# Clipping the feed-forward weights on GpSimd instead of VectorE inside one attention tile

## The chip, the cores and the metric

The kernel runs on one core of one Trainium2 chip. The metric is the time of one execution on the device in microseconds; lower is better. The time before is the median of three runs.

## The reference, cut to what matters

One transformer-like layer over x of 16 sequences × 64 tokens × 256: cross attention with 16 heads to a context of 256 tokens per sequence, then a selective-scan (Mamba) layer, then a gated feed-forward layer whose weights are quantised to −1, 0, 1. The change touches only how those weights are prepared.

```python
def _weight_quant(w):
    scale = 1.0 / jnp.clip(jnp.mean(jnp.abs(w)), 1e-05)
    wq = jnp.clip(jnp.round(w * scale), -1.0, 1.0) / scale
    return w + jax.lax.stop_gradient(wq - w)
...
gate = jax.nn.silu(_bitlinear(x, w_gate))      # w_gate, w_up: 1024 x 256
up = _bitlinear(x, w_up)
return _bitlinear(gate * up, w_down)           # w_down: 256 x 1024
...
x = x + _L0_xattn_ref(_layernorm(x, axis=-1), ctx_1024, ...)
x = x + _L0_attn_ref(_layernorm(x, axis=-1), ...)
x = x + _L0_ffn_ref(_layernorm(x, axis=-1), L0_ffn_w_gate, L0_ffn_w_up, L0_ffn_w_down)
```

## The kernel before

The program is written out by hand: each engine has its own instruction queue, run strictly in order, and semaphores tie the queues together. There are three stages. In the first, eight attention tiles (t = 0 to 7) of 128 tokens each run one after the other; in the second, the selective scan runs over 64 half units (GpSimd's `weigh`, VectorE's `scan`); in the third, the feed-forward layer runs over eight tiles.

An attention tile has eight units (u = 0 to 7), two heads for two sequences each. The work of one unit goes round the engines:

- TensorE computes the scores (`scores`, L496), VectorE masks them and takes the largest (`mask_scores`, L1425), ScalarE takes the exponential and its sum (`exps`, L1016), VectorE inverts the sums (`invert_sums`, L1432) one unit later.
- GpSimd multiplies the probabilities by the inverse (`normalise`, L1843), two instructions of 128x256 for each unit. TensorE turns them (`turn_probs`, L513), also one unit later; VectorE or ScalarE copies them to SBUF (`copy_pt`, L1437 and L1022), TensorE multiplies them with the values (`values`, L531).

Between the units each queue has other work at fixed places: on TensorE the keys (`keys`, L544), queries and values of the next tile, the projection of the previous one (`project`, L584) and the turn of its normalised output (`scan_in`, L596). The first key projection of the next tile is issued at unit 0, which is what marks a tile's start in the text. On VectorE stand the layer norms' statistics (L1373, L1377) and second halves (`ln_second`, L1381), in which GpSimd computes the inverse deviation between the two (`rstds`, L1826 and L1829). `rstds` stands before the normalise of unit 2, 4 and 6. GpSimd also adds the bias of the projection (`add_bias`, L1836) and the residual (`pool_resid`, L1864) at unit 6.

The feed-forward weights are three arrays of 128x2048 float32 in SBUF (`wraw`). They are prepared in the shadow of the attention, in six halves of 128x1024, one half behind each of units 1 to 6 of a tile: absolute sums on ScalarE in tile 2 (`W_SUM`), the mean in tile 3, scaling and rounding (adding MAGIC) on ScalarE in tile 4 (`scale_weights`, L1069), the clip in tile 5 (`W_CLIP`, `clip_weights`, L1532), the conversion to bfloat16 on ScalarE in tile 6 (`weights_to_bf16`, L1074). Before the scan stage, several queues wait for all six conversions (`w_step`).

Of the kernel before, what the change touches and what calls it, by code (L numbers as in the profile page):

```python
# [17 lines left out]
ALU = mybir.AluOpType  # L18
# [24 lines left out]
MAGIC = 12582912.0  # L43
# [27 lines left out]
W_SUM, W_MEAN, W_SCALE, W_CLIP, W_BF16 = 2, 3, 4, 5, 6  # L71
# [35 lines left out]
def build(nc, x, ctx_t, mask, wq, wkv, wproj, bproj, vecs, cons, win, wall, wout, wg, wu, wd, out):  # L107
    with ExitStack() as ctx:
# [5 lines left out]
        def sem(name, by=None):  # L114

            s = ctx.enter_context(nc.semaphore(name))
            if by is not None:
                from_one[by].append(s)  # L120
            return s
# [50 lines left out]
        def first_use(at, n):  # L172
            return both[:, at:at + n]
# [8 lines left out]
        wraw = [first_use(16384 + 2048 * n, 2048) for n in range(3)]  # L182
# [38 lines left out]
        HALF_W = KD * FI // 2  # L221

        def half_of(w, n):
            return w[:, HALF_W * n:HALF_W * (n + 1)]
# [75 lines left out]
        w_scaled, w_clipped = sem("w_scaled"), sem("w_clipped")  # L300
# [49 lines left out]
        def lagged(tile, u, lag, first, fn, only=None):  # L350

            v = u - lag
            if v >= UNITS or v < 0 and first:
                return
            if only is None or v % UNITS in only:
                fn(tile if v >= 0 else tile.step(-1), v % UNITS)
# [632 lines left out]
        def _(act):  # L989
# [80 lines left out]

            def weights_to_bf16(n):

                act.wait_ge(w_clipped, n + 1)
                act.activation(half_of(wq3[n // 2], n % 2), half_of(wraw[n // 2], n % 2), ACT.Copy, bias=-MAGIC  # L1074
                               ).then_inc(w_step, 1)

# [284 lines left out]
        def _(dve):  # L1361
# [6 lines left out]
            def ln_first(n, tile, src, src_sem, src_val):  # L1368

                if src_sem is not None:  # L1370
                    dve.wait_ge(src_sem, count(src_val))
                dve.wait_ge(ln_mv[n], count(tile.t))
                dve.bn_stats(stats[n][:], src).then_inc(ln_stats[n], 1)  # L1373
                dve.wait_ge(ln_rstd[n], count(tile.t))
                dve.wait_ge(ln_stats[n], count(tile.t + 1))
                dve.sem_inc(passed, 1)
                dve.bn_aggr(meanvar[n][:], stats[n][:]).then_inc(ln_mv[n], 1)  # L1377
# [26 lines left out]
            def copy_vals(tile):  # L1404
                dve.wait_ge(v_ready[1], count(tile.t + 1))
                dve.wait_ge(pv_done, count(tile.t * 2 - 2))
                dve.tensor_copy(v_sb[:, tile.par, 1].rearrange("p k d -> p (k d)"), bank(6)).then_inc(v_in_sb[1], 1)
# [9 lines left out]
            def mask_scores(tile, u):  # L1417

                dve.wait_ge(s_ready, count(tile.t * 8 + (u + 1)))
                if u == 0:  # L1420
                    dve.wait_ge(maskf_ready, count(tile.t + 1))
                dve.wait_ge(pt_ready, count(tile.t * 8 + (u - 7)))
                dve.sem_inc(passed, 1)
                for q in range(2):
                    dve.tensor_tensor_reduce(sm[:, u, q * LK:(q + 1) * LK], score_bank(tile, u)[:, q * LK:(q + 1) * LK],  # L1425
                                             maskf[:, tile.par, q * LK:(q + 1) * LK], 1.0, HUGE, ALU.add,
                                             ALU.min, negmax[:, u, q:q + 1]).then_inc(masked, 1)
# [38 lines left out]
            def body(tile, first, last):  # L1466
                nxt, prev = tile.step(1), tile.step(-1)
                for u in range(UNITS):
                    if last:
                        if u % 2 == 0 and u:  # L1470
                            mask_scores(tile, u)
                            mask_scores(tile, u + 1)
                    else:
                        if u in MASK_AT:
                            for v in MASK_AT[u]:
                                mask_scores(tile, v)
                        if u == UNITS - 1:
                            mask_scores(nxt, 0)
                            if nxt.last():
                                mask_scores(nxt, 1)  # L1480
                    lagged(tile, u, LAG_INVERT, first, invert_sums)
                    lagged(tile, u, LAG_COPY_ODD, first, copy_pt, (1, 3, 5, 7))
                    if first and u == 0:
                        copy_vals(tile)
                        dve.wait_ge(loaded, N_LOADED)
                    if not last:
                        if u == DVE_LN1_FIRST:
                            ln_first(0, nxt, x_of(nxt), None, 0)
                        if u == DVE_LN1_SECOND:
                            ln1_second(nxt)  # L1490
                        if u == DVE_KEYS:
                            copy_keys(nxt)
                        if u == DVE_QUERIES:
                            copy_queries(nxt)
                        if u == DVE_VALS:
                            copy_vals(nxt)
                    if not first:
                        if u == DVE_PICK_HEADS + last:
                            pick_heads(prev)
                        if u == DVE_ADD_PROJ + last:  # L1500
                            add_proj(prev)
                        if u == DVE_NORM_Y1 + last:
                            norm_y1(prev)
                        if u == DVE_NORM_Z:
                            norm_z(prev)
                    if u == DVE_MASK and not last:
                        make_mask(nxt)
                    if last:
                        for c in range(NC):
                            if u == CONVOLVE_AT[c]:  # L1510
                                convolve(0, c)
                    if first and u == 6:
                        late_constants()
                    if tile.t == W_MEAN and u == 5:
                        dve.wait_ge(w_sum, 1)
                        dve.tensor_copy(wpart[:], bank(4)[:, 0:6]).then_inc(w_mean, 1)
                        dve.wait_ge(w_mean, 1)
                        dve.tensor_reduce(wmean[:], wpart[:].rearrange("p (n h) -> p n h", h=2), AX, ALU.add
                                          ).then_inc(w_mean, 1)
                        dve.wait_ge(w_mean, 2)  # L1520
                        dve.tensor_scalar(wmean[:], wmean[:], 1.0 / (D * FI), EPS, ALU.mult, ALU.max
                                          ).then_inc(w_mean, 1)
                        dve.wait_ge(w_mean, 3)
                        dve.reciprocal(winv[:], wmean[:]).then_inc(w_inv, 1)
                    if tile.t == W_CLIP and 1 <= u <= 6:
                        clip_weights(u - 1)

            def clip_weights(n):

                dve.wait_ge(w_scaled, n + 1)  # L1530
                part = half_of(wraw[n // 2], n % 2)
                dve.tensor_scalar(part, part, MAGIC + 1.0, MAGIC - 1.0, ALU.min, ALU.max  # L1532
                                  ).then_inc(w_clipped, 1)

            def late_constants():
                dve.tensor_copy(identb[:], ident).then_inc(consts, 1)
# [284 lines left out]
        def _(pool):  # L1821
# [16 lines left out]
            def normalise(tile, u):  # L1838
                pool.wait_ge(rden_ready, count(tile.t * 8 + (u + 1)))
                pool.sem_inc(passed, 1)  # L1840
                for q in range(2):
                    s = sm[:, u, q * LK:(q + 1) * LK]
                    pool.tensor_scalar(s, s, rden[:, u, q:q + 1], 1.0, ALU.mult, ALU.mult).then_inc(normed, 1)  # L1843

            def body(tile, first, last):
                nxt, prev = tile.step(1), tile.step(-1)
                for u in range(UNITS):
                    if u == POOL_RSTD0 and not last:
                        rstds(0, nxt)
                    if u == 2 and first:  # L1850
                        pool.wait_ge(loaded, N_LOADED)
                        add_bias(tile)
                    if u == POOL_BIAS and not last:
                        add_bias(nxt)
                    if u == POOL_RSTD1 and not first:
                        rstds(1, prev)
                    if u == POOL_RSTD2 + last and not first:
                        rstds(2, prev)
                        pool_resid(prev)
                    normalise(tile, u)  # L1860

            def pool_resid(tile):
                pool.wait_ge(ln_out[1], count(tile.t + 1))
# [214 lines left out]
```

## Time and profile before

| what | before |
|---|---|
| runs: median (lowest to highest) | 410.5 us (409.54 to 410.86) |
| profiled execution: span, its own time | 410.8 us, 412.68 us |
| TensorE matmuls busy | 361.4 us (88%) |
| VectorE busy | 348.2 us (85%) |
| ScalarE busy | 278.7 us (68%) |
| GpSimd busy | 285.5 us (69%) |
| mean granted clock of TensorE | 0.992 |

The span is from the first to the last instruction of the profiled execution; its own time includes what lies around them. Busy times are means over the whole span, with stages of quite different limits: the attention takes the first 180 us or so, the scan goes on to some 365 us, and the feed-forward layer follows.

### The profile page before, as it was taken

The numbers are of one execution on the slowest core, as the hardware profiler recorded it, in microseconds if no ns is written. First come the engines' busy times: TensorE is split into PE (matmuls) and PEld (weight loads), VectorE is DVE, ScalarE is ACT, GpSimd is POOL, SyncE is SP. The second block draws the span as 40 slices with busy tenths as digits, with TensorE's granted clock in tenths as the row PEclk, the third lists the DMA queues.
The fourth block names the chain that finished last, engine by engine and source line by source line (L and its number), as shares of the span: only waits on it lengthen the run. The fifth ranks groups of instructions, "written<-read, shape, count | busy, mean of one in ns | idle before, by whom it ended". The sixth has DMA issues, their size and how long they took to land.

```text
span 410.8 us, 8698 instructions
## 1 busy us (share of the span) xinstructions
PE 361.4 (88%) x2886; PEld 246.2 (60%) x2886; DVE 348.2 (85%) x723; ACT 278.7 (68%) x596; POOL 285.5 (69%) x333
## 2 busy tenths in 40 slices
PE   7899999999998999887798999898889778889774
PEld 5556767676776765453465566566576656557442
DVE  1558888797989778958989999989999999988795
ACT  1267589769966993489569879857874554266574
POOL 0056475565657472248999999999999699986830
PEclk9999999999999999999699999999999999999999
DMA  7981010110100000019400001364000000000001
GB/s 209 357 360 53 2 51 14 42 51 3 53 2 0 2 3 0 2 38 249 128 2 0 2 4 26 92 191 129 2 1 2 1 2 0 2 0 2 14 26 65
DMA packets 23039, 22.41 MB, mean 55 GB/s; under 512 B 1074, under 2 KB 20914, under 8 KB 22484
## 3 DMA queue, kind: packets, MB, share of 16 engines
q1 hardware_dynamic: 22436, 21.39, 16.7%
q8 instruction: 23, 0.38, 0.4%
q10 hardware_dynamic: 560, 0.48, 0.4%
q14 instruction: 20, 0.16, 0.1%
HBM read 20.75 MB, written 1.12 MB: 53 GB/s over the span
## 4 chain that ended last, share of the span: by engine, by line
PE 28%; DVE 20%; ACT 17%; POOL 17%; issue 16%; DMA 1%; DVEq 0%; PEld 0%; POOLq 0%; SPq 0%; ACTq 0%; PEldq 0%
POOL both L1897 12%; PE ps L544 7%; ACT both L1181 5%; DVE both L1601 4%; PE ps L513 4%; PE ps L496 3%; DVE both L1425 2%; PE ps L531 2%; PE ps L607 2%; PE ps L574 2%; ACT both L1016 2%; PE ps L759 2%; PE ps L561 2%; DVE f_s L1693 1%; ACT both L1167 1%
## 5 line engine op out<-in xcount | busy, mean ns | idle before, releaser
L1897 POOL TENSOR_TENSOR both<-both 128x1024 f32<-128x1024 f32 x64 | 150.4, 2386 | 2.4 <-DVE both L1601 1.8
L1601 DVE TENSOR_TENSOR_SCAN both<-both,ps 128x1024 f32<-128x1024 f32 x64 | 143.0, 2271 | 5.6 <-PE ps L749 5.5
L1843 POOL TENSOR_SCALAR both<-both,rden 128x256 f32<-128x256 f32 x128 | 61.7, 497 | 62.8 <-DVE rden L1432 62.6
L1181 ACT ACTIVATE both<-delta,a_neg 128x504 f32<-128x504 f32 x120 | 74.8, 704 | 12.3 <-DVE both L1601 12.2
L759 PE MATMUL ps<-con,both 128*128 128x128 f32 x512 | 72.5, 281 | 7.5 <-POOL both L1897 7.4
L759 PEld LDWEIGHTS ps<-con,both 128*128 128x128 f32 x512 | 56.8, 142 | 29.5 <-issue 16.3
L1016 ACT ACTIVATE both<-both,negmax 128x256 f32<-128x256 f32 x128 | 63.3, 498 | 15.7 <-DVE negmax L1425 15.7
L749 PE MATMUL ps<-both 32*128 32x256 f32 x512 | 46.7, 435 | 11.7 <-DVE both L1601 9.6
L1425 DVE CUSTOM_DVE_ANT_0 both<-ps,both 128x256 f32<-128x256 f32 x128 | 46.9, 417 | 6.7 <-PE ps L496 5.5
L513 PEld LDWEIGHTS ps<-con,both 128*128 128x128 f32 x256 | 30.6, 141 | 12.7 <-issue 8.0
L513 PE MATMUL ps<-con,both 128*128 128x128 f32 x256 | 38.2, 275 | 0.0
L749 PEld LDWEIGHTS ps<-both 32*128 32x128 f32 x512 | 20.5, 186 | 27.6 <-DVE both L1601 15.5
L544 PE MATMUL ps<-both 128*128 128x512 f32 x64 | 33.0, 640 | 2.7 <-DMA both<-in_wkv 1.3
L574 PE MATMUL ps<-both 128*128 128x256 f32 x128 | 31.1, 387 | 0.5 <-DVE both L1400 0.5
L1437 DVE COPY both<-ps 128x512 f32<-128x512 f32 x32 | 21.6, 676 | 10.2 <-PE ps L513 10.2
L1022 ACT ACTIVATE both<-ps 128x512 f32<-128x512 f32 x32 | 18.8, 588 | 14.6 <-PE ps L513 14.6
L574 PEld LDWEIGHTS ps<-both 128*128 128x128 f32 x128 | 23.1, 190 | 6.0 <-issue 2.7
L1016 ACT ACTIVATION_READ_ACCUMULATOR both<-both,negmax 128x1 f32 x128 | 24.5, 191 | 0.0
L1826 POOL TENSOR_TENSOR vareps<-meanvar,eps 128x1 f32<-128x1 f32 x24 | 6.3, 261 | 25.5 <-DVE meanvar L1377 25.5
L496 PE MATMUL ps<-both 32*128 32x256 f32 x256 | 20.6, 399 | 3.0 <-DVE negmax L1425 2.0
L544 PEld LDWEIGHTS ps<-both 128*128 128x128 f32 x64 | 11.3, 197 | 14.9 <-issue 13.0
L496 PEld LDWEIGHTS ps<-both 32*128 32x128 f32 x256 | 13.2, 184 | 8.3 <-issue 6.7
(151 smaller groups left out, 616.7 us busy)
## 6 DMA issues: line engine op xcount, KB each, us to landing
both<-bounce SPq DMA_DIRECT2D x16, 512.0 KB, 6.4
both<-in_ctx_t SPq DMA_DIRECT2D x8, 512.0 KB, 3.4
both<-in_wg SPq DMA_DIRECT2D x1, 1024.0 KB, 8.9
both<-in_wu SPq DMA_DIRECT2D x1, 1024.0 KB, 10.6
both<-in_wd SPq DMA_DIRECT2D x1, 1024.0 KB, 12.6
win_sb<-in_win SPq DMA_DIRECT2D x1, 1024.0 KB, 13.8
resid<-in_x SPq DMA_DIRECT2D x1, 896.0 KB, 6.3
both<-in_wkv SPq DMA_DIRECT2D x2, 256.0 KB, 3.4
```

The lines of the kernel that those rows point to most:

```text
L496: mm = pe.matmul(score_bank(tile, v)[:, bb * LK:(bb + 1) * LK], q2[rows, tile.par, hf, bb].rearrange("p r q -> p (r q)"), kt_sb[rows, tile ...
L513: tr = pe.transpose(pt_bank(tile, u)[:, (q * 2 + kt) * P:(q * 2 + kt + 1) * P], sm[:, u, q * LK + kt * P:q * LK + (kt + 1) * P], ident)
L544: mm = pe.matmul(kv_bank(tile, hf), wkv_sb[:, k, hf * P:(hf + 1) * P], ctx_sb[:, tile.par, k], start=k == 0, stop=k == KD - 1)
L574: mm = pe.matmul(kv_bank(tile, 1 - bb)[:, kt * D:(kt + 1) * D], ctx_sb[:, tile.par, k, bb * LK + kt * P:bb * LK + (kt + 1) * P], wkv_sb[:, ...
L749: mm = pe.matmul(bank(inflow_bank(hu) + sq).rearrange("p (n h t) -> p n h t", n=HN, h=2)[:, :, th], ut[rows, e.idx % 2, tt], bd[rows, e.nh ...
L759: mm = pe.matmul(bank(Y_BANK)[:, e.tt * P:(e.tt + 1) * P], g_sb[:, hu % RING_G, n * P:(n + 1) * P], ident, start=False, stop=e.nh == NH - ...
L1016: act.activation(s, s, ACT.Exp, scale=-1.0, bias=negmax[:, u, q:q + 1], accum_out=den[:, u, q:q + 1]).then_inc(expd, 1)
L1181: act.activation(da[sl % 2].rearrange("p (a s n t) -> p a s n t", a=GT, n=HN, s=2)[:, :, :, n, 1:L], delta[:, idx % RING_D].rearrange("p ( ...
L1425: dve.tensor_tensor_reduce(sm[:, u, q * LK:(q + 1) * LK], score_bank(tile, u)[:, q * LK:(q + 1) * LK], maskf[:, tile.par, q * LK:(q + 1) * ...
L1601: dve.tensor_tensor_scan(h_sb[:, hu % RING_H], da[e.slot % 2][:, e.tt * HU:(e.tt + 1) * HU], bank(inflow_bank(hu), 2), 0.0, ALU.mult, ALU. ...
L1843: pool.tensor_scalar(s, s, rden[:, u, q:q + 1], 1.0, ALU.mult, ALU.mult).then_inc(normed, 1)
L1897: pool.tensor_tensor(g_sb[:, hu % RING_G].rearrange("p (n s t) -> p s n t", n=HN, s=2), h_sb[:, hu % RING_H].rearrange("p (s n t) -> p s n ...
```

## The change

VectorE no longer clips. GpSimd does, behind its normalise of units 1 to 6 of the same tile (5). Each half of 1024 columns is clipped by two instructions of 512 columns, so the semaphore `w_clipped` counts 12 instead of 6, and ScalarE waits for twice the count plus two. The arithmetic is the same.

```diff
             def weights_to_bf16(n):
 
-                act.wait_ge(w_clipped, n + 1)
+                act.wait_ge(w_clipped, 2 * n + 2)
...
-                    if tile.t == W_CLIP and 1 <= u <= 6:
-                        clip_weights(u - 1)
-
-            def clip_weights(n):
-
-                dve.wait_ge(w_scaled, n + 1)
-                part = half_of(wraw[n // 2], n % 2)
-                dve.tensor_scalar(part, part, MAGIC + 1.0, MAGIC - 1.0, ALU.min, ALU.max
-                                  ).then_inc(w_clipped, 1)
...
                     normalise(tile, u)
+                    if tile.t == W_CLIP and 1 <= u <= 6:
+                        clip_weights(u - 1)
+
+            def clip_weights(n):
+
+                pool.wait_ge(w_scaled, n + 1)
+                part = half_of(wraw[n // 2], n % 2)
+                for q in range(2):
+                    quarter = part[:, HALF_W // 2 * q:HALF_W // 2 * (q + 1)]
+                    pool.tensor_scalar(quarter, quarter, MAGIC + 1.0, MAGIC - 1.0, ALU.min, ALU.max
+                                       ).then_inc(w_clipped, 1)
```

## Rows read from the trace of the kernel before

**Rows 1.** The page's first part: busy time, share of the span, instructions.

```profile
PE 361.4 (88%) x2886; PEld 246.2 (60%) x2886; DVE 348.2 (85%) x723; ACT 278.7 (68%) x596; POOL 285.5 (69%) x333
```

**Rows 2.** Windows, tiles 4 and 5: length, busy PE PEld DVE ACT POOL, clock, DMA.

```profile
93.05:112.01 18.96, 18.23 (x169) 13.09 (x169) 16.01 (x62) 18.16 (x48) 11.42 (x25) 1.00 0.10 30
112.01:132.04 20.03, 18.26 (x169) 13.12 (x169) 18.67 (x68) 12.61 (x42) 12.90 (x24) 1.00 0.01 1
```

**Rows 3.** VectorE's clip by source line: duration in ns min/median/max, first and last start.

```profile
L1532 DVE TENSOR_SCALAR both<-both x6: 659/668/1219, 113.0 to 127.7; 128x1024 f32<-128x1024 f32 x6
```

**Rows 4.** The chain of waits in tile 5: start us, us on it, what.

```profile
119.82 0.68 DVE both L1532
...
123.00 0.38 DVE both L1532
...
125.08 0.59 DVE both L1532
...
127.79 0.35 DVE both L1532
```

**Rows 5.** GpSimd's timeline, tile 5 and start of 6: start us, us, [idle before, releaser].

```profile
113.30 2.09 POOL L1843 TENSOR_SCALAR both<-both,rden 128x256 f32<-128x256 f32 x4 [0.42 <-DVE rden L1432]
115.86 0.54 POOL L1826 TENSOR_TENSOR vareps<-meanvar,eps 128x1 f32<-128x1 f32 x1 [0.47 <-DVE meanvar L1377]
...
120.78 0.93 POOL L1843 TENSOR_SCALAR both<-both,rden 128x256 f32<-128x256 f32 x2 [1.84 <-DVE rden L1432]
...
127.42 0.90 POOL L1836 TENSOR_TENSOR resid<-resid,both 128x256 f32<-128x256 f32 x1
...
129.00 0.55 POOL L1829 TENSOR_TENSOR rstd<-vareps,neg_half 128x1 f32<-128x1 f32 x1
129.52 0.73 POOL L1864 TENSOR_TENSOR resid<-y,z 128x256 f32<-128x256 f32 x1
...
132.21 0.93 POOL L1843 TENSOR_SCALAR both<-both,rden 128x256 f32<-128x256 f32 x2 [0.94 <-DVE rden L1432]
...
135.89 0.19 POOL L1826 TENSOR_TENSOR vareps<-meanvar,eps 128x1 f32<-128x1 f32 x1 [0.50 <-DVE meanvar L1377]
```

**Rows 6.** VectorE's timeline in tile 5.

```profile
122.87 0.18 DVE L1377 BATCH_NORM_AGGREGATE meanvar<-stats 128x2 f32<-128x6 f32 x1
...
124.92 0.08 DVE L1425 DVE_READ_ACCUMULATOR2_ANT negmax<- 128x1 f32 x1
...
127.65 1.22 DVE L1532 TENSOR_SCALAR both<-both 128x1024 f32<-128x1024 f32 x1
```

**Rows 7.** TensorE's timeline where tile 5 ends and tile 6 begins.

```profile
130.61 0.44 PE L596 MATMUL ps<-con,xn 128*128 128x128 f32 x2 [0.94 <-DVE xn L1381]
...
132.04 1.95 PE L544 MATMUL ps<-both 128*128 128x512 f32 x4
133.83 0.60 PE L513 MATMUL ps<-con,both 128*128 128x128 f32 x4
```

**Rows 8.** GpSimd's two-operation instructions by source line: ns min/median/max, starts, forms.

```profile
L1843 POOL TENSOR_SCALAR both<-both,rden x128: 471/478/736, 20.5 to 177.8; 128x256 f32<-128x256 f32 x128
...
L1965 POOL TENSOR_SCALAR xnt<-xnt,f_s x5: 474/478/481, 369.8 to 392.1; 128x256 f32<-128x256 f32 x5
...
L1938 POOL TENSOR_SCALAR dtb<-xnt x8: 1065/1070/1537, 340.3 to 392.7; 128x256 bf16<-128x256 f32 x8
...
L1932 POOL TENSOR_SCALAR xnt<-resid,f_s x5: 1217/1218/1219, 366.9 to 387.9; 128x256 f32<-128x256 f32 x5
```

**Rows 9.** Groups of GpSimd by form: one column, and two inputs of 504 columns.

```profile
L1906 POOL TENSOR_TENSOR xc<-xc,zst 128x504 f32<-128x504 f32 x4 | 5.1, 1263 | 0.0
...
L1921 POOL TENSOR_SCALAR f_nmean<-f_s 128x1 f32<-128x1 f32 x3 | 0.8, 265 | 0.3
```

**Rows 10.** Windows of the stretch where TensorE's granted clock falls.

```profile
188.00:192.00 4.00, 1.63 (x12) 0.54 (x10) 3.76 (x6) 4.00 (x12) 3.43 (x7) 1.00 1.07 286
...
196.00:200.00 4.00, 1.88 (x11) 1.23 (x12) 4.00 (x3) 1.76 (x4) 3.94 (x2) 0.70 0.88 237
```

## The prediction, made before the change was run

> **What bounds the kernel now.** I read the page's busy shares first: no engine is saturated over the span; TensorE and VectorE lead and GpSimd stands at 69% [rows 1]. That share is a mean, and the change lives in one attention tile, so I cut the span there: from one tile's first key projection to the next is 18.96 us in tile 4 and 20.03 us in tile 5, the clip tile [rows 2]. TensorE does the same 18.2 us of work in both; what differs is VectorE, 16.01 us busy against 18.67. The chain of waits says why: four of the six clips stand on it in tile 5, for 0.68, 0.38, 0.59 and 0.35 us, 2.0 us together [rows 4]. So VectorE's clips do set the pace of tile 5, and the most that their removal can give there is about what tile 5 has over tile 4, 20.03 − 18.96 = 1.07 us. Then I read the timeline of the engine that gets the work. GpSimd is busy 12.90 of tile 5's 20.03 us [rows 2], so it has 7.1 us free, in gaps of 0.4 to 1.8 us where it waits for VectorE [rows 5]. Last, TensorE at the seam: its turn of the probabilities of unit 7 starts at 133.83, and GpSimd's normalise of that unit ends at 132.21 + 0.93 = 133.14 [rows 5, 7]. That is the slack of GpSimd at the seam: 0.7 us. Whatever pushes that normalise more than 0.7 us delays TensorE, and with it tile 6 and everything behind it, because every engine's queue runs in order and the attention tiles lead into the scan.
>
> **What is removed.** Six clips on VectorE, 668 ns each in the median, one of 1219 [rows 3]. That one starts at 127.65, while GpSimd's add of the bias runs from 127.42 to 128.32 [rows 5, 6], so some 0.6 us of it is waiting for that instruction. The reverse is seen too: GpSimd's one-column add at 115.86 takes 0.54 us against 0.19 at 135.89 in tile 6, where there is no clip [rows 5]. Both losses go. The Trainium skill ("SBUF — State Buffer", section "Who interferes with whom") says that GpSimd and a VectorE instruction in a two-port mode exclude each other for a whole instruction; the trace agrees with that here, and by it VectorE's short SBUF-to-SBUF instructions could now wait behind a clip piece. I cost that at nothing, since the sum below has VectorE ahead of GpSimd anyway.
>
> **What is added.** Twelve instructions on GpSimd, 128x512 float32 in place, minimum then maximum with two constants, a pair behind the normalise of each of units 1 to 6. No such form is in the trace, so I bound it. Four forms with two operations on 256 columns stand there: multiply then multiply, 478 ns; multiply then add, 478 ns; subtract then minimum, constants, bfloat16 out, 1070 ns; subtract then multiply, 1218 ns [rows 8]. One column takes 265 ns [rows 9], which I take as the fixed part. Doubling the rest: 265 + 2 × 213 = 691 ns on the fast forms, 265 + 2 × 805 = 1875 ns and 265 + 2 × 953 = 2171 ns on the slow ones. The fast forms hold only multiply and add. The only one with a minimum, and the only one with two constants, is slow. So I take the slow side, between its two: 2.0 us a piece, 4.0 us a pair, 24 us in all, and keep 0.69 us as the other end.
>
> The Trainium skill speaks against this choice ("GPSIMD Engine Reference", section 3.1, "Elementwise — side-by-side cycle accounting"): a loop body with at most two operations is bound by its port at 1.03 cycles per element. My estimate from that page of the Trainium skill is 512 × 1.03 / 1.2 GHz = 440 ns and a start, near the fast end. The trace agrees for multiply with multiply or add and disagrees for the two forms that begin with subtract.
>
> **The sum.** Behind the clip of unit 1, GpSimd's queue holds, until unit 7 is normalised: six normalises of 0.93, three steps of inverse deviation of 0.82 (0.19 + 0.55 and the gaps between), the bias add without its collision, 0.73, and the residual add, 0.73 [rows 5]: 9.5 us. Normalise 1 ends at 113.30 + 2.09 = 115.39 [rows 5]. With 24 us of clips GpSimd never waits for VectorE, since 33.5 us of work lies where 17.75 passed before: normalise 7 ends at 115.39 + 9.5 + 24.0 = 148.9 instead of 133.14, +15.8. The slack takes 0.7; the small stops of TensorE at the start of tile 6 give back perhaps 0.3 (my guess, the size of one such stop). Net +14.8 us. What is queued behind each pair: the inverse deviation for the next layer norm, for which VectorE waits with its copies behind it; the next normalise, for which TensorE waits with the scores, values and keys behind it. The relief of VectorE gives nothing, as VectorE then waits for GpSimd.
>
> ScalarE's conversion to bfloat16 is in tile 6 and its wait is for clips that stand in GpSimd's queue ahead of normalise 7; the scaling before them is over in tile 4. Both waits are met: nothing. No DMA is moved.
>
> The profiled execution has a span of 410.8 us and took 412.68; the median of the runs is 410.5. The step is added to any of them: span 425.6, and 410.5 + 14.8 = 425.3 us in the runs.
>
> The ends: pieces of 1.875 us give 12 × 0.125 = 1.5 us less, 423.8; pieces of 2.171 give 2.0 more, 427.4. One more cost is open. The granted clock is 1.00 in tile 5 and 0.70 (a mix of the two levels, 1.2 and 2.4 GHz) in 196 to 200 us, after a stretch in which TensorE was busy 1.63 of 4.00 us [rows 2, 10]. With 18.3 us of matmuls spread over 35 us it may fall here too. Most of that is covered by the waits for GpSimd; uncovered, 4 us of work at half speed is 4 us. So this case's own range is 422 to 431.
>
> **Rivals.**
> *Fast pieces* (0.69 us, 8.3 us in all). Then GpSimd still meets VectorE: the statistics for the second inverse deviation are ready at 123.05 as now (they hang on TensorE's projection), and the sums for normalise 4 at 124.92 + 0.08 less one clip, 0.6, at 124.4 [rows 6]. From there it runs without a gap: four normalises 3.7, three pairs 4.1, bias, inverse deviation and residual 2.3, so normalise 7 ends at 134.5, +1.4; less 0.7 of slack, +0.7 us: 411.2. It is 0.2% over, which counts as no change. Its doubt is some 0.8 us, so it can also come out slower by over 0.3%.
>
> *Middle pieces.* If the form runs at the pace of two inputs, 1263 ns for 504 columns [rows 9], a piece is 1.28 us, 15.4 us in all: normalise 7 ends at 140.3, +7.1, less 1.0: 416.6. Nothing speaks for it but that such a pace exists on this engine.
>
> *Faster.* VectorE is relieved and GpSimd's added work stays hidden: tile 5 shrinks to tile 4's length, −1.07 us, 409.4; if TensorE's stop at 130.61 for VectorE (0.94) [rows 7] and the others go wholly, 408.9. By the count above this decides where from 124.4 on the 6.0 us of other work and three pairs end before 133.83 − 1.07 = 132.8: pairs of at most 0.8 us, pieces of 0.4. That is below the fastest row for half as many columns, so this case needs GpSimd's order to have slack that I haven't seen (the bias add could be late with no harm, say).
>
> **How the numbers follow.** Slow pieces 0.70, middle 0.10, fast 0.16, faster 0.04. The predicted time is that of the slow pieces, 425.3. The range for 8 in 10 reaches over the middle case to the fast one: 411 to 431. A measurement of this kernel tells about 0.3% (1.2 us) from no change. Slow and middle are slower by over 0.3%, and of the fast case 0.03: 0.83. No change: 0.13 of the fast case less a hundredth, 0.12. Faster: 0.04 and that hundredth, 0.05.
>
> **What would show it.** In the profile after: the new line's median, 1.9 to 2.2 us against 0.7; GpSimd busy from 115.4 without a gap to 149; the distance of the key projections of tiles 5 and 6, some 34 to 35 us against 20.03; TensorE waiting for GpSimd's normalise in each unit of tile 5; tile 6 and the scan as long as before. The prediction is wrong if minimum and maximum are fast forms, which a single row tells, or if the delay of tile 5 is given back later. If pieces are slow and the time rises by much less than 15 us, then it is the claim of order and slack that failed.

## The result, and the profile after

The changed kernel takes 414.95 us (median of 6 runs, 412.9 to 416.4), the kernel before 410.86 beside it; ratio 1.0095, 95% interval 1.0066 to 1.0124. It is slower, as forecast, but by 4 us and not by 15: 414.95 lies in my range of 411 to 431 and far from its centre, 425.3. It lies nearest to the middle rival's 416.6, by chance: no piece costs what that rival took.

The page of the changed kernel, span and busy shares, answering to [rows 1]:

```profile
span 413.4 us, 8700 instructions
...
PE 364.7 (88%) x2882; PEld 247.8 (60%) x2886; DVE 345.7 (84%) x717; ACT 278.8 (67%) x596; POOL 291.7 (71%) x345
```

The new line by source, which is the row that decides my price, and the window from the first key projection of tile 5 to that of tile 6, answering to [rows 2]:

```profile
L1861 POOL TENSOR_SCALAR both<-both x12: 614/614/665, 115.0 to 133.7; 128x512 f32<-128x512 f32 x12
```

```profile
111.82:134.06 22.24, 18.75 (x168) 13.95 (x169) 16.48 (x62) 13.02 (x44) 18.42 (x36) 0.96 0.00 1
```

A piece takes 614 ns. I had taken 2.0 us. Tile 5 grew from 20.03 to 22.24 us. VectorE's work in it fell from 18.67 to 16.48 us, as it should; GpSimd's rose from 12.90 to 18.42.

GpSimd's timeline in the second half of tile 5, answering to [rows 5]:

```profile
125.85 1.36 POOL L1861 TENSOR_SCALAR both<-both 128x512 f32<-128x512 f32 x2
127.31 0.94 POOL L1834 TENSOR_SCALAR both<-both,rden 128x256 f32<-128x256 f32 x2
128.34 1.31 POOL L1861 TENSOR_SCALAR both<-both 128x512 f32<-128x512 f32 x2
129.73 0.72 POOL L1827 TENSOR_TENSOR resid<-resid,both 128x256 f32<-128x256 f32 x1
...
130.68 0.55 POOL L1820 TENSOR_TENSOR rstd<-vareps,neg_half 128x1 f32<-128x1 f32 x1
...
134.37 2.77 POOL L1834 TENSOR_SCALAR both<-both,rden 128x256 f32<-128x256 f32 x6
```

VectorE, which makes the statistics for that inverse deviation and then waits for it, and TensorE, which waits for VectorE, answering to [rows 6] and [rows 7]:

```profile
126.01 0.18 DVE L1377 BATCH_NORM_AGGREGATE meanvar<-stats 128x2 f32<-128x6 f32 x1
...
131.34 0.73 DVE L1381 TENSOR_SCALAR xn<-z,meanvar,rstd 128x256 f32<-128x256 f32 x1 [2.98 <-POOL rstd L1820]
```

The same instruction in the kernel before:

```profile
130.15 0.41 DVE L1381 TENSOR_SCALAR xn<-z,meanvar,rstd 128x256 f32<-128x256 f32 x1
```

TensorE in the changed kernel:

```profile
127.96 1.08 PE L531 MATMUL ps<-both 128*32 128x128 f32 x32
132.12 0.44 PE L596 MATMUL ps<-con,xn 128*128 128x128 f32 x2 [3.08 <-DVE xn L1381]
132.40 1.87 PE L513 MATMUL ps<-con,both 128*128 128x128 f32 x8
134.06 2.77 PE L544 MATMUL ps<-both 128*128 128x512 f32 x4
136.67 0.60 PE L513 MATMUL ps<-con,both 128*128 128x128 f32 x4
```

The inverse deviation ends at 131.23 where it ended at 129.55. Its statistics had been ready since 126.19 (127.43 before); the rest of one clip pair, a normalise, a second clip pair and the bias add stood ahead of it. TensorE's stop there grew from 0.94 to 3.08 us, of which 0.6 us is that TensorE came to it earlier; the turned output comes 1.5 us later. Then the matmuls themselves are longer: eight turns take 1.87 us against 1.10, four key projections 2.77 against 1.95. The windows of the changed kernel say why; the last three columns are the granted clock, the DMA share and GB/s:

```profile
128.00:132.00 4.00, 1.04 (x33) 0.77 (x32) 1.02 (x3) 1.57 (x5) 3.67 (x8) 1.00 0.00 0
132.00:136.00 4.00, 3.88 (x13) 2.85 (x14) 2.96 (x17) 2.30 (x7) 3.74 (x8) 0.57 0.00 0
...
392.00:396.00 4.00, 3.01 (x13) 1.83 (x15) 3.76 (x9) 1.23 (x2) 1.88 (x5) 0.50 0.19 66
```

In this execution, after TensorE was busy 1.04 of 4 us, the clock is mostly at its lower level, 1.2 GHz, for the next 4 us. In the kernel before it stays at 1.00 there. A second stretch, in the feed-forward layer, has a low clock too, where the profile of before shows 1.00. From the first to the last of that layer's eight `largest` instructions (the reduction of VectorE that finds each tile's largest value) it is 41.0 us against 39.2.

### The profile page after: what moved, and what is told of

The parts are those of the page before. It is cut to its first block, busy times and chain, and to the rows that moved or that the text cites. A ratio compares the mean times of both kernels' runs of the same rounds, so it can differ in the third digit from the quotient of the medians.

```text
span 413.4 us, 8700 instructions
## 1 busy us (share of the span) xinstructions
PE 364.7 (88%) x2882; PEld 247.8 (60%) x2886; DVE 345.7 (84%) x717; ACT 278.8 (67%) x596; POOL 291.7 (71%) x345
## 4 chain that ended last, share of the span: by engine, by line
PE 33%; DVE 19%; POOL 18%; issue 15%; ACT 13%; DMA 1%; DVEq 0%; PEld 0%; POOLq 0%; SPq 0%; ACTq 0%; PEldq 0%
POOL both L1899 11%; PE ps L544 7%; DVE both L1592 5%; ACT both L1181 4%; PE ps L513 4%; PE ps L496 3%; PE ps L759 2%; PE ps L531 2%; PE ps L749 2%; PE ps L561 2%; DVE both L1425 2%; PE ps L574 2%; ACT both L1016 2%; PE ps L837 1%; POOL dtb L1940 1%
## 5 line engine op out<-in xcount | busy, mean ns | idle before, releaser
L1817 POOL TENSOR_TENSOR vareps<-meanvar,eps 128x1 f32<-128x1 f32 x24 | 5.2, 216 | 25.4 <-DVE meanvar L1377 25.1
L544 PEld LDWEIGHTS ps<-both 128*128 128x128 f32 x64 | 11.8, 205 | 15.0 <-issue 13.3
```

The source lines that it names most:

```text
L544: mm = pe.matmul(kv_bank(tile, hf), wkv_sb[:, k, hf * P:(hf + 1) * P], ctx_sb[:, tile.par, k], start=k == 0, stop=k == KD - 1)
```

## The experiments

The profiles give three marks that I use throughout: the length of tile 5 (first key projection to the next), the start of the first scan instruction, and the length of the feed-forward layer (first to last start of `largest`). Tile 5 itself starts anywhere from 110.8 to 112.5 us in these profiles, so the table also gives the first scan counted from that start.

| kernel | ratio to before | median us | tile 5 | first scan | the same, from tile 5's start | feed-forward |
|---|---|---|---|---|---|---|
| before | 1 | 409.8 to 410.9 | 20.03 | 188.6 | 76.6 | 39.2 |
| changed | 1.0095 | 414.95 | 22.24 | 191.5 | 79.7 | 41.0 |
| e1_forms | – | one run, 426.99 | 21.74 | 189.9 | 78.4 | 39.2 |
| e2_late | 1.0041 | 412.1 | 20.24 | 189.9 | 78.1 | 39.3 |
| e3_warm | 1.0087 | 414.13 | 23.10 | 191.8 | 79.7 | 39.9 |
| e4_relief | 0.9966 | 409.43 | 18.74 | 187.7 | 75.3 | 39.3 |
| e5_warm10 | 1.0041 | 412.33 | 21.74 | 190.7 | 78.4 | 39.2 |
| e6_load | 1.0129 | 416.01 | 23.95 | 192.8 | 82.0 | 39.9 |
| e7_slow | 1.0327 | 423.72 | 31.96 | 201.4 | 90.1 | 39.2 |
| e8_gaps | 0.9949 | 408.58 | 18.72 | 187.1 | 75.2 | 39.3 |
| e9_again | – | one run, 412.75 | 20.04 | 188.7 | 76.6 | 39.3 |
| e10_shift19 | 1.0097 | 413.6 | 22.74 | 190.3 | 79.3 | 39.3 |
| e11_shift32 | 1.0154 | 416.11 | 25.64 | 194.7 | 82.2 | 39.2 |

The medians of the kernel before lay at 410.58, 410.38 and 409.83 us beside the three timed groups.

### e1_forms: what makes a GpSimd form slow

```diff
             scale_output(7)
+            src, at = both[:, 0:512], [4096]
+            def form(cols, a, b, op0, op1, dt=F32):
+                for _ in range(2):
...
+                    pool.tensor_scalar(dst, src[:, 0:cols], a, b, op0, op1)
+            form(512, 0.5, -0.5, ALU.min, ALU.max)
+            form(256, 0.5, -0.5, ALU.min, ALU.max)
+            form(512, 0.5, -0.5, ALU.mult, ALU.mult)
+            form(512, 0.5, 0.25, ALU.subtract, ALU.min)
+            form(256, 0.5, 0.25, ALU.subtract, ALU.min)
+            form(256, 0.5, 0.25, ALU.subtract, ALU.min, BF16)
+            form(256, 0.5, 0.25, ALU.min, ALU.max, BF16)
+            form(512, 0.5, 0.25, ALU.subtract, ALU.mult)
+            form(256, eps[:, 0:1], neg_half[:, 0:1], ALU.subtract, ALU.mult)
+            form(256, eps[:, 0:1], neg_half[:, 0:1], ALU.mult, ALU.mult)
+            form(256, 0.5, 0.25, ALU.add, ALU.mult)
+            form(256, 0.5, 0.25, ALU.min, ALU.subtract)
```

> The changed kernel with 24 GpSimd tensor_scalar instructions of twelve forms, each twice, added behind the last instruction of GpSimd's queue, where it has nothing more to do; they read scan data and write regions that nobody reads. Theory A (what makes a form slow is a subtract as first operation): min,max on 512 columns 614 ns as in the changed kernel and some 400 to 480 ns on 256; mult,mult on 512 about 690; every form that begins with subtract slow, 1000 ns or more on 256 columns and 1800 or more on 512, constants or columns as scalars; min then subtract slow too; bfloat16 output changes nothing for min,max. Theory B (the bfloat16 output made line 1938 slow, and the two columns as scalars made line 1932 slow): subtract,min to float32 is fast, min,max to bfloat16 slow, and mult,mult with two columns slow.

GpSimd's timeline at its end, one row for each form in the order of the diff, start and length in us:

```profile
402.73 0.61 POOL L2033 TENSOR_SCALAR both<-both 128x512 f32<-128x512 f32 x1
...
403.90 0.40 POOL L2033 TENSOR_SCALAR both<-both 128x256 f32<-128x256 f32 x1
...
404.62 0.80 POOL L2033 TENSOR_SCALAR both<-both 128x512 f32<-128x512 f32 x1
...
406.14 1.92 POOL L2033 TENSOR_SCALAR both<-both 128x512 f32<-128x512 f32 x1
...
409.91 1.06 POOL L2033 TENSOR_SCALAR both<-both 128x256 f32<-128x256 f32 x1
...
411.98 1.06 POOL L2033 TENSOR_SCALAR both<-both 128x256 bf16<-128x256 f32 x1
...
414.04 0.40 POOL L2033 TENSOR_SCALAR both<-both 128x256 bf16<-128x256 f32 x1
...
414.77 1.92 POOL L2033 TENSOR_SCALAR both<-both 128x512 f32<-128x512 f32 x1
...
418.58 1.21 POOL L2033 TENSOR_SCALAR both<-both,eps,neg_half 128x256 f32<-128x256 f32 x1
...
420.99 0.55 POOL L2033 TENSOR_SCALAR both<-both,eps,neg_half 128x256 f32<-128x256 f32 x1
...
422.06 0.40 POOL L2033 TENSOR_SCALAR both<-both 128x256 f32<-128x256 f32 x1
...
422.80 1.08 POOL L2033 TENSOR_SCALAR both<-both 128x256 f32<-128x256 f32 x1
```

Theory A holds but for a size. Subtract makes a form slow, in either place: 1.92 us on 512 columns, 1.06 to 1.21 on 256. Minimum, maximum, multiply and add are fast, 0.61 to 0.80 and 0.40 to 0.55, though two multiplies took 0.80 us on 512 columns where 0.69 was expected, more than minimum and maximum. A bfloat16 output costs nothing. Subtract and multiply with columns for scalars took 0.15 us more on 256 columns than subtract and minimum with constants; on 512 columns, with constants, the two pairs took the same, so the columns are the likely reason. No pair was timed both ways.

### e2_late: the same load, two pairs later

```diff
-                    if tile.t == W_CLIP and 1 <= u <= 6:
+                    if tile.t == W_CLIP and 1 <= u <= 4:
                         clip_weights(u - 1)
+                    if tile.t == W_CLIP and u == 7:
+                        clip_weights(4)
+                        clip_weights(5)
```

> The changed kernel with the clip pairs 4 and 5 (those behind units 5 and 6) moved behind the normalise of unit 7. The same work on GpSimd, but nothing of it ahead of the last inverse deviation. Theory A (the loss is one late step: the inverse deviation behind two clip pairs makes TensorE stop 3.1 us, and the clock falls for it): that inverse deviation is done by about 129.9 instead of 131.2, TensorE's stop ahead of the turned normalised output shrinks from 3.1 to under 1.9 us, the granted clock stays 1.00 in tile 5, the distance of the key projections of tiles 5 and 6 falls from 22.2 to about 19.5 us, and the time is within 0.4% of before, ratio 0.996 to 1.004. Theory B (8.4 us more of GpSimd work cost by themselves, by contention for the port or a later normalise): the ratio stays at 1.006 or more.

Ratio 1.0041, interval 1.0018 to 1.0064. The inverse deviation ends at 129.77 and the clock is 1.00, as theory A had it. Tile 5 is 20.24 us, 0.7 over what it gave, and the ratio lies just outside its window, which ended at 1.004; theory B's 1.006 or more is just inside the interval. TensorE's timeline:

```profile
130.66 0.44 PE L596 MATMUL ps<-con,xn 128*128 128x128 f32 x2 [1.58 <-DVE xn L1381]
...
140.08 0.41 PE L553 MATMUL ps<-con,both 128*128 128x128 f32 x2 [1.16 <-DVE both L1394]
```

The stop in tile 5 is 1.58 us instead of 3.08, but another appears in tile 6, where there was none. GpSimd's timeline in e2_late shows its cause, and VectorE's the wait between the two:

```profile
133.28 2.70 POOL L1864 TENSOR_SCALAR both<-both 128x512 f32<-128x512 f32 x4
...
138.17 0.55 POOL L1820 TENSOR_TENSOR rstd<-vareps,neg_half 128x1 f32<-128x1 f32 x1
```

```profile
138.84 0.50 DVE L1381 TENSOR_SCALAR both<-resid,meanvar,rstd 128x256 f32<-128x256 f32 x1 [1.41 <-POOL rstd L1820]
```

The moved clips make the next tile's first inverse deviation late, done at 138.72 where it was done at 136.71. It is the same mechanism in another place: 0.2 us more in tile 5 and 1.16 us in tile 6 make up nearly all of this run's 1.5 us.

### e3_warm and e5_warm10: the stop without the clock's fall

```diff
             def scan_in(tile):
+                if tile.t == W_CLIP - 1:
+                    pe.wait_ge(v_in_sb[1], count(tile.t + 3))
+                    for _ in range(20):
+                        pe.matmul(bank(6)[:, 0:P], ident, ident, start=True, stop=True)
```

> The changed kernel with 20 matmuls of 128x128 on the identity, about 2.4 us, put into TensorE's stop of 3.1 us ahead of the turn of the normalised output in tile 5; they write a bank that the turn then overwrites. No other work is touched, and GpSimd is as late as in the changed kernel. Theory A (about half of tile 5's loss is the clock that falls because TensorE stops): the granted clock stays 1.00 from 132 to 136 us, the next key projections take 1.95 us instead of 2.77, the turn of eight 1.1 instead of 1.87, the seam moves from +2.8 to about +1.4 us against before, and the time falls by 1 to 2 us against the changed kernel, ratio to before 1.003 to 1.007. Theory B (the clock there is covered by waits): the seam and the time are those of the changed kernel, ratio about 1.0095.

> The changed kernel with 10 matmuls of 128x128 on the identity in TensorE's stop, half of the run before this one, whose filler took 4.7 us instead of the 2.4 expected and so delayed TensorE by itself. These take about 2.4 us and fit in the stop of 3.1 us. Theory A (half of tile 5's loss is the fallen clock): clock 1.00 from 132 to 136 us, the turned output at 132.1 as in the changed kernel, the next key projections 1.96 us, the seam 1.3 to 1.5 us earlier than in the changed kernel; time 1 to 2 us below it, ratio 1.004 to 1.007. Theory B (the clock is covered): seam and time as in the changed kernel, 1.0095.

The 20 matmuls took 4.73 us: each counts as two in the profile. That delayed TensorE itself, so e3_warm's ratio of 1.0087 (1.0059 to 1.0115) misses theory A's window and tells nothing of the clock's price; it shows only that the clock stayed at 1.00 and the key projections took 1.96 us. e5_warm10, the same edit with range(10), is the clean one. TensorE's timeline in it, and its window:

```profile
128.50 1.08 PE L531 MATMUL ps<-both 128*32 128x128 f32 x32
...
132.94 1.19 PE L513 MATMUL ps<-con,both 128*128 128x128 f32 x8
134.09 1.96 PE L544 MATMUL ps<-both 128*128 128x512 f32 x4
135.91 0.66 PE L513 MATMUL ps<-con,both 128*128 128x128 f32 x4
```

```profile
132.00:136.00 4.00, 3.34 (x16) 1.83 (x16) 3.48 (x17) 2.27 (x7) 3.74 (x8) 1.00 0.00 0
```

From the values (L531) to the eight turns it is 4.44 us in both kernels, so GpSimd is as late. From there to the turn of unit 7 it is 4.27 us in the changed kernel (132.40 to 136.67) and 2.97 here: 1.3 us are the fallen clock. The ratio is 1.0041, interval 1.0021 to 1.0062, within theory A's window. It fell by more than 1.3 us (0.54%, 2.2 us): in the profile the feed-forward layer is 39.2 us, not 41.0.

The trace of e1_forms bears on this too, as its program is that of the changed kernel up to the added forms. TensorE's timeline and window in it:

```profile
131.81 0.44 PE L596 MATMUL ps<-con,xn 128*128 128x128 f32 x2 [3.08 <-DVE xn L1381]
132.08 1.19 PE L513 MATMUL ps<-con,both 128*128 128x128 f32 x8
...
135.05 0.65 PE L513 MATMUL ps<-con,both 128*128 128x128 f32 x4
```

```profile
132.00:136.00 4.00, 4.00 (x26) 2.32 (x29) 2.87 (x17) 3.04 (x9) 3.74 (x9) 1.00 0.00 0
```

The stop is the same 3.08 us, with 0.92 us of work from 128 to 132 us, and the clock does not fall, with nothing filled in. So the stop makes a fall possible and not certain, and one profile cannot say that the filler prevented it. The price is confirmed: 2.97 us from the eight turns to unit 7's, and the first scan 78.4 us behind tile 5's start against 79.7, 1.3 us less for the same code. That the fall is common in the changed kernel and rare in e5_warm10 rests on the mean clocks of their runs, which hold falls elsewhere too: 0.978 to 0.983 in five of six, against 0.988 to 0.995 in all twelve.

### e4_relief and e6_load: each half of the change alone

e4_relief leaves the clips out on both engines; e6_load keeps VectorE's clips and has GpSimd repeat each in two pieces of 512 (`clip_again`, minimum and maximum, once VectorE's is done).

```diff
# e4_relief, against the changed kernel
-                act.wait_ge(w_clipped, 2 * n + 2)
+                act.wait_ge(w_scaled, n + 1)
...
-                    if tile.t == W_CLIP and 1 <= u <= 6:
-                        clip_weights(u - 1)
# e6_load, against the kernel before
                     normalise(tile, u)
+                    if tile.t == W_CLIP and 1 <= u <= 6:
+                        clip_again(u - 1)
...
```

In e6_load ScalarE's conversion waits for GpSimd's repeated clips.

> The clips are left out altogether: neither VectorE nor GpSimd clips, so the weights are not limited to -1 to 1. It shows what VectorE's relief alone is worth. My prediction's term: tile 5 becomes as long as tile 4, 19.0 us instead of 20.0, and the time falls by 1.07 us, ratio 0.997. Theory B (the relief is swallowed later, in the scan, whose start waits on transfers and ScalarE): tile 5 shortens and the ratio is 1.000.

> The kernel before, VectorE's clips kept, and GpSimd repeats each of them in two pieces of 512 behind the same normalise as in the change (it clips what is clipped already). The load alone, without VectorE's relief. Theory A: GpSimd's last inverse deviation is as late as in the changed kernel or later, TensorE stops 3 us or more and the clock falls; tile 5 is 22.5 to 24 us, the ratio 1.010 to 1.014, the change's own loss plus up to the 1.07 us of relief. Theory B (VectorE's relief is worth nothing once GpSimd is late, since VectorE only waits for it): the ratio is that of the changed kernel, 1.0095.

Relief alone: tile 5 18.74 us, ratio 0.9966 (0.9943 to 0.9989), as my bound of 1.07 us had it (1.15 us measured; the interval spans 0.5 to 2.3 us, and tile 5 is 1.3 us shorter). Load alone: tile 5 23.95 us, TensorE's stop 3.66 us, ratio 1.0129 (1.0099 to 1.0158), inside theory A's window. The product is that of the whole change, 1.0129 × 0.9966 = 1.0095, though the load is not quite the same: beside VectorE's clips, several of GpSimd's instructions were longer (two clip pairs took 1.63 and 1.69 us against 1.31, the normalises of one unit 1.50 against 0.94), and the clock fell further, so that the key projections took 3.46 us against 2.77.

### e7_slow: the price that I forecast

```diff
-                    pool.tensor_scalar(quarter, quarter, MAGIC + 1.0, MAGIC - 1.0, ALU.min, ALU.max
+                    pool.tensor_scalar(quarter, quarter, 0.0, MAGIC + 1.0, ALU.subtract, ALU.min
```

> The changed kernel with another pair of operations in the clips: subtract 0, then minimum with the upper bound. The lower bound is left out, so values below -1 stay. The instruction costs 1.92 us for 512 columns where min,max costs 0.61. It puts the price that I forecast into the changed kernel and tests the other terms of my sum. Theory A (only the price was wrong): GpSimd runs without a gap from 115 to about 148 us, the normalise of unit 7 ends at 147 to 149, the key projections of tiles 5 and 6 lie 33 to 36 us apart, and the time is 421 to 428. Theory B (the sum's order and slack were wrong too, the delay is given back): below 418.

423.72 us, ratio 1.0327 (1.0289 to 1.0364); rows of GpSimd's and TensorE's timelines:

```profile
114.39 3.81 POOL L1861 TENSOR_SCALAR both<-both 128x512 f32<-128x512 f32 x2
...
145.58 2.74 POOL L1834 TENSOR_SCALAR both<-both,rden 128x256 f32<-128x256 f32 x6
```

```profile
141.06 0.69 PE L596 MATMUL ps<-con,xn 128*128 128x128 f32 x2 [8.99 <-DVE xn L1381]
...
143.25 2.55 PE L544 MATMUL ps<-both 128*128 128x512 f32 x4
146.56 0.66 PE L513 MATMUL ps<-con,both 128*128 128x128 f32 x4 [0.77 <-POOL both L1834]
```

GpSimd runs without a gap, normalise 7 ends at 145.58 + 0.93 = 146.5, and the median is 13.3 us over before. My sum with pairs of 3.79 us (0.2 less than I took, 1.3 in all) gives 14.8 − 1.3 = 13.5. Here TensorE's turn of unit 7 does wait for that normalise, 0.77 us, as the sum has it, so the low clock ahead of it is covered. Tile 5 is 32.0 us, below the 33 that I had named, since part of the delay falls behind the seam, and normalise 7 ends just below the 147. Theory A holds in the time.

### e8_gaps: the clips where GpSimd waits

```diff
-                    if tile.t == W_CLIP and 1 <= u <= 6:
-                        clip_weights(u - 1)
+                    if u in (2, 3) and W_SCALE <= tile.t <= W_BF16:
+                        clip_weights(2 * (tile.t - W_SCALE) + u - 2)
```

> The changed kernel with the six clip pairs spread over tiles 4, 5 and 6, two in each, behind the normalise of units 2 and 3, where GpSimd waits 1.4 to 1.9 us for VectorE. Theory A (GpSimd's price fits in its gaps, and what costs is only what it makes late): no inverse deviation is late, TensorE has no stop over 1 us there, VectorE keeps its relief of 1.07 us, and the time comes to that of the kernel without clips, ratio 0.996 to 0.999. Theory B (each pair costs wherever it stands, by the shared port or the next normalise): the ratio is 1.001 or more.

408.58 us, ratio 0.9949, interval 0.9929 to 0.9969: faster than both kernels, and a little more so than theory A's 0.996. GpSimd's pairs in tile 5, and TensorE at its end:

```profile
118.43 1.31 POOL L1861 TENSOR_SCALAR both<-both 128x512 f32<-128x512 f32 x2
120.05 0.94 POOL L1834 TENSOR_SCALAR both<-both,rden 128x256 f32<-128x256 f32 x2 [0.31 <-DVE rden L1432]
121.07 1.31 POOL L1861 TENSOR_SCALAR both<-both 128x512 f32<-128x512 f32 x2
122.88 0.19 POOL L1817 TENSOR_TENSOR vareps<-meanvar,eps 128x1 f32<-128x1 f32 x1 [0.50 <-DVE meanvar L1377]
```

```profile
129.16 0.44 PE L596 MATMUL ps<-con,xn 128*128 128x128 f32 x2 [0.20 <-DVE xn L1381]
```

Both pairs fit: GpSimd still waits for VectorE behind each (0.31 and 0.50 us). TensorE's stop is 0.20 us, and tile 5 is 18.72 us. The ratio is as good as without any clips, so in these places the clips on GpSimd cost nothing that the runs can show.

### e9_again, e10_shift19, e11_shift32: the clock elsewhere

e9_again is the kernel before, unchanged. The other two are e8_gaps with the filler of e3_warm, 19 matmuls (the diff) and 32.

```diff
             def scan_in(tile):
+                if tile.t == W_CLIP - 1:
+                    pe.wait_ge(v_in_sb[1], count(tile.t + 3))
+                    for _ in range(19):
+                        pe.matmul(bank(6)[:, 0:P], ident, ident, start=True, stop=True)
```

> The kernel before, unchanged, profiled once more. The profiled execution that the prediction rests on took 412.7 us, 2.2 us more than the median of its runs, and its scan stage (first to last scan's start) took 167.8 us, while in all seven profiles of changed kernels it took 165.6 to 165.8. Theory A (that execution's scan stage was 2 us longer than usual, because TensorE's clock fell at another point): this profile shows 165.6 to 165.8 us for that stage, and a time of 410 to 411 us. Theory B (the scan stage of the kernel before is longer, and the change gives 2 us there): 167.5 us or more again.

> The kernel with the clips in the gaps, plus 19 matmuls on the identity in TensorE's queue in tile 5, which keep TensorE busy for 4.5 us. Everything behind comes 4.5 us later than there, 3.1 us later than in the kernel before, the delay of the changed kernel, but no wait and no fall of the clock in tile 5 goes with it. It asks where the rest of the changed kernel's loss comes from: its feed-forward layer took 41.0 us from the first to the last largest value, others took 39.2. Theory A (only the point in time decides: when that layer starts 3 us late, the clock falls in it): 39.9 to 41.0 us here too, clock under 0.9 in 390 to 400 us, and the median 3.8 to 4.5 us over before, ratio about 1.010. Theory B (the fall there hangs on what happened in tile 5): 39.2 to 39.3 us, and 3.1 us over before, ratio 1.0075.

> The same with 32 matmuls, 7.6 us, so the rest comes 6.2 us later than in the kernel before. Theory A: another point in time, so the feed-forward layer's clock may be whole again as in the slow-form run (13 us late, 39.2 us), ratio about 1.015; with a fall there 1.019. Theory B: 39.2 us and ratio 1.015.

e9_again: 412.75 us while the run beside it took 410.17, and again 167.8 us from the first to the last scan; VectorE's scan by source line in its trace:

```profile
L1601 DVE TENSOR_TENSOR_SCAN both<-both,ps x64: 2256/2275/2289, 188.7 to 356.5; 128x1024 f32<-128x1024 f32 x64
```

Theory B's sign came, 167.5 us or more again. But VectorE's timeline in the same trace, where the clock is 0.71, 0.50 and 0.94 in the three windows from 196 to 208 us, shows where the 2 us lie:

```profile
201.85 4.46 DVE L1601 TENSOR_TENSOR_SCAN both<-both,ps 128x1024 f32<-128x1024 f32 x2 [0.90 <-PE ps L749]
207.37 0.73 DVE L1557 SCALAR_TENSOR_TENSOR xc<-ps,vec,xc 128x496 f32<-128x496 f32 x1 [1.06 <-ACT zst L1114]
```

Both profiles of the kernel before have these two waits, 1.96 us together. In the changed kernel's profile the low clock lies from 192 to 204 us and VectorE is busy all 4.00 of every 4 us from 192 to 212. So the 2 us go with where the clock falls, as theory A said, though that repeats itself in the profiled executions. They aren't the usual ones: of 53 runs of the kernel before in these groups, the 16 with a mean clock of 1.000 have a median of 409.45 us and the 10 with 0.982 or 0.983 one of 412.3. The six runs of the changed kernel have 0.978 to 0.988. So the profiles differ by less (2.5 us, 415.20 against 412.68) than the medians (4.1), and how often the clock falls is part of what is timed. That the scan stage of the usual run is shorter wasn't seen, as those runs have no trace; it is inferred from the medians.

e10_shift19 (ratio 1.0097, interval 1.0077 to 1.0116) did not show a fall in the feed-forward layer: its profile has a mean clock of 1.000, a clock of 1.00 in that layer, and 39.3 us there. e11_shift32 neither: 39.2 us, ratio 1.0154 (1.0138 to 1.0170). That speaks against theory A, but the other runs of e10 have a clock of 0.988, and its ratio is A's, so the pair settles nothing. Its profile shows 2.7 us at the first scan, counted from tile 5's start, and its median is 3.8 us over before.

## Why the prediction was off

- **The bound.** Right. VectorE's clips were worth 1.07 us of tile 5 as read; 1.15 us measured alone (e4_relief).
- **The price of a piece.** This is the step that failed: "The only one with a minimum, and the only one with two constants, is slow. So I take the slow side". Taken 2.0 us a piece and 24 us in all, measured 0.614 and 7.4. Line 1938 is slow for its subtract and for nothing else (e1_forms). The four rows allowed two readings, "min is slow" and "subtract is slow"; both slow forms began with subtract, and both fast ones lacked it. With the right price my own working gives 411.2 us, no change. I had the rule of the Trainium skill ("GPSIMD Engine Reference", section 3.1) against me and set it aside. My estimate from it, 440 ns and a start, agrees with the 614 ns; the rule fails for subtract, 1.92 us on the same 512 columns.
- **The rest of the sum.** Order, 9.5 us of other work, 0.7 us of slack: right. With the slow price in the kernel the time rose by 13.3 us where the sum gives 13.5 (e7_slow). That holds where GpSimd never waits; at the real price the slack at unit 7 isn't what decides.
- **The fast rival.** It said 411.2, and 414.95 came. Its timeline was nearly right: normalise 7 to end at 134.5, measured 134.37 + 0.93 = 135.3. I looked for the damage at the normalise of unit 7 and charged 0.7 us; in the changed kernel that normalise was done 1.4 us before TensorE came to it (136.67). The late step was the inverse deviation before it, which I never followed to TensorE: it came at 131.23, 1.7 us later than before, and TensorE stops until then. I had no term for that stop, nor for the clock, so that the kernel came out slower, as forecast, is luck: it did so by a path that is in none of my sums. By the profile: the turned output comes 1.5 us later (132.12 against 130.61), the low clock costs 1.3 us more at the seam (e5_warm10), and the first scan starts 2.9 us later (191.5 against 188.6). Where the clock did not fall, in e1_forms, the first scan is 1.8 us later, counted from tile 5's start. I had named the clock as a risk of the slow case only.
- **Contention for the port.** Costed at nothing, and nearly right. VectorE's `ln_second` at 131.34 took 0.73 us beside GpSimd's residual add, where the same instruction took 0.41 us before, at 130.15; so 0.3 of the 1.5 us by which the turned output is late are this collision. It isn't the twelve pieces that collide there, and it was 0.75 us one tile earlier, at 109.55, in the kernel before. e8_gaps, with the twelve pieces on GpSimd and the same 0.76 us there, is no slower than e4_relief with none.
- **Given back later?** No. The medians move by as much as the first scan does, counted from tile 5's start, within 0.5 us in e2_late, e3_warm, e4_relief, e5_warm10, e6_load, e7_slow and e8_gaps. In the changed kernel, e10_shift19 and e11_shift32 they move by 0.7 to 1.1 us more.
- **Open.** In medians the change costs 4.1 us, of which the profile has 3.1 at the first scan, counted from tile 5's start. The rest may be the clock's fall in the feed-forward layer (41.0 us against 39.2 in the profile); that is argued and not shown. The fall there isn't fixed to the change: in e1_forms, the same code, that layer takes 39.2 us at a clock of 1.00. What decides in which executions the clock falls, there or after the stop, is not settled.

## What to carry to other kernels

Before an operation is moved to GpSimd, look for its own pair of operations in the trace, and where it isn't there, time that pair alone: the same instruction with another pair of operations took three times as long. Then lay the moved work into the queue's timeline and look for the first step behind it that another engine waits for; that an engine has enough free time in the tile says little, and two placements of the same twelve instructions differed by 1.5%. A later step costs TensorE what it is late by and, in the executions in which the clock falls, the slow matmuls behind it. Compare more than one profile before a difference of 1 or 2 us is put down to a change: here two executions of the same code differed by 1.3 us at the first scan, with the clock.

## What the runs showed of the hardware

- GpSimd's two-operation form on 512 float32 columns: 0.61 us for minimum and maximum, 0.80 for two multiplies, 1.92 with a subtract in it. Adding a negated constant may therefore be faster than subtracting (on 256 columns add with multiply took 0.40 us, subtract with minimum 1.06); such a replacement in this kernel wasn't tried.
- TensorE stopped for 3.08 us with 1.04 us of work in the 4 us around it, and the clock averaged 0.57 in the next 4 us. In another execution of the same code (e1_forms) the stop was the same, with 0.92 us of work, and the clock stayed at 1.00. The stops of 0.94 and 1.58 us, and the one filled by matmuls, brought no fall in tile 5 in their profiles.
- One kernel's runs spread over 4 us, and partly with the mean clock: a median of 409.45 us at 1.000 and 412.3 at 0.982 or 0.983, but anything from 409.5 to 412.9 at 0.992.
